# Spreading ScalarE's work over a recurrence, and a sum of powers by another identity

## The reference, cut to what matters

```python
# layer 0, feed-forward: a recurrence over t (3136 steps), all 64 images at once
yt = jax.nn.sigmoid(wx_t + yt @ Vt)
# layer 1, mixer
forget_gate = jax.nn.sigmoid(x_ri @ Wf + bf + 2.0)
input_gate = jax.nn.sigmoid(x_ri @ Wi + bi)
delta = jax.nn.softplus(x_ri @ Wd + bd) * 0.1
scale = 0.95 * jax.nn.sigmoid(mag) / (mag + 1e-08)   # |A| <= 0.95
inp_r = delta[..., :c] * input_gate[..., :c] * Bx_r   # inp_i likewise
def step(h_state, _):                                 # 16 times, h0 = 0
    h_r, h_i = h_state
    Ah_r = Ar * h_r - Ai * h_i
    Ah_i = Ar * h_i + Ai * h_r
    return ((fg_r * Ah_r + inp_r, fg_i * Ah_i + inp_i), None)
```

## Time and profile before

| | |
|---|---|
| time, median of 3 runs (lowest, highest) | 14605.63 us (14566.55, 14616.49) |
| the profiled execution's own time | 14537.58 us |
| its span | 14535.8 us |
| busy: PE, PEld, DVE, ACT, POOL | 79%, 60%, 76%, 68%, 28% |
| granted clock of TensorE, mean | 0.81 |

### The profile page before, as it was taken

How to read it: one execution, slowest core, us unless ns; L and a number is a source line. 1 busy time by engine, 2 the same in 40 slices (tenths; PEclk the granted TensorE clock), 3 DMA queues, 4 the chain that set the end, 5 groups by cost and what they waited for, 6 DMA issues and landing times. The chain is left out here.

```text
span 14535.8 us, 248087 instructions
## 1 busy us (share of the span) xinstructions
PE 11419.5 (79%) x87538; PEld 8744.4 (60%) x87538; DVE 11053.6 (76%) x22880; ACT 9833.3 (68%) x22679; POOL 4012.8 (28%) x3975
## 2 busy tenths in 40 slices
PE   7888888888888867777777777777777547776998
PEld 5666666666666645555555555555555235555888
DVE  6777777777777718999999999999999965554133
ACT  6888888888888846666666666667666567776100
POOL 5444444445444421212111211112121111211000
PEclk9999999999999967777777777777777677777555
DMA  3333333333333321111111111111111133333599
GB/s 69 86 81 82 81 82 87 76 90 73 90 77 86 75 61 41 53 53 53 51 47 52 53 53 53 51 46 53 53 52 40 23 84 94 99 90 89 172 316 309
DMA packets 1967708, 1189.72 MB, mean 82 GB/s; under 512 B 48853, under 2 KB 1900056, under 8 KB 1958436
## 3 DMA queue, kind: packets, MB, share of 16 engines
q1 hardware_dynamic: 1554148, 967.87, 26.3%
q10 hardware_dynamic: 408832, 205.55, 5.0%
q0 software_dynamic: 3648, 2.20, 0.1%
HBM read 708.85 MB, written 466.62 MB: 81 GB/s over the span
## 5 line engine op out<-in xcount | busy, mean ns | idle before, releaser
L1236 PEld LDWEIGHTS s_pW<-s_XU,s_vh 128*128 128x128 f32 x6272 | 1415.7, 261 | 1969.1 <-ACT s_XU L1107 1699.7
L1236 PE MATMUL s_pW<-s_XU,s_vh 128*128 128x64 f32 x6272 | 1493.2, 331 | 1071.4 <-ACT s_XU L1107 1071.4
L1107 ACT ACTIVATE s_XU<-s_pW,s_zb 128x64 f32<-128x64 f32 x3136 | 995.7, 318 | 1788.7 <-PE s_pW L1236 1738.1
L1265 PE MATMUL s_pG<-s_wg,s_XNT 128*128 128x384 f32 (+1 forms) x3200 | 1506.0, 559 | 37.5 <-ACT s_Z L1086 37.5
L832 POOL TENSOR_TENSOR s_rst<-s_var,s_epst 128x16 f32<-128x16 f32 (+1 forms) x100 | 141.7, 1417 | 3906.6 <-DVE s_var L79 3906.6
L408 ACT ACTIVATE KB<-pV,qkb 32x392 f32<-32x392 f32 x2048 | 1190.5, 581 | 25.0 <-PE pV L498 1.1
L248 POOL TENSOR_TENSOR SS<-SS,mx 128x784 f32<-128x784 f32 x512 | 769.5, 1503 | 804.8 <-DVE mx L341 804.6
L1203 PEld LDWEIGHTS s_pY<-s_hident,s_XU 128*128 128x128 f32 (+1 forms) x3200 | 752.2, 305 | 177.7 <-issue 129.6
L1711 PE MATMUL c_pS<-c_OX,c_Wm 64*112 64x128 f32 x3584 | 737.6, 420 | 91.1 <-DVE c_X L1727 76.6
L460 ACT ACTIVATE XH<-XR,nm,rs 112x128 f32<-112x128 f32 x1792 | 733.6, 485 | 92.1 <-POOL nm L267 83.6
L506 PE MATMUL pS<-KB,QT 128*64 128x196 f32 x8192 | 793.7, 336 | 0.0
(11 more groups left out here) (249 smaller groups left out, 31958.3 us busy)
## 6 DMA issues: line engine op xcount, KB each, us to landing
XL<-in_x_dram SPq DMA_DIRECT2D x64, 1568.0 KB, 12.4
XR<-in_x_dram SPq DMA_DIRECT2D x64, 1568.0 KB, 18.0
x_dram<-XR SPq DMA_DIRECT2D x64, 1568.0 KB, 8.1
xh_dram<-XH SPq DMA_DIRECT2D x64, 1568.0 KB, 8.1
r_X<-x_dram SPq DMA_DIRECT2D x64, 1568.0 KB, 14.2
c_X<-x_dram SPq DMA_DIRECT2D x64, 1568.0 KB, 19.4
out_dram<-c_X ACTq DMA_DIRECT2D x64, 1568.0 KB, 13.9
s_XQ<-xh_dram ACTq DMA_DIRECT2D x384, 256.0 KB, 2.8
```

The source lines that it names most:

```text
L1107: act.activation(XU[j % 2][:, t, :], pW[t // R % 2][:, B * (t % R):B * (t % R) + B], ACT.Tanh, bias=zb[:, 0:1], scale=0.5).then_inc(u_sb, 1)
L1236: pe.matmul(pW[t // R % 2][:, B * (t % R):B * (t % R) + B], vh[:], before, start=False, stop=True, skip_group_check=True).then_inc(z_ps, 1)
L1265: pe.matmul(pG[i % 3][0:tc, 0:3 * C], XNT[:, i, 0:tc], wg[:], start=True, stop=True).then_inc(g_ps, 1)
```

## The change

It touches `scan_phase` alone.

1. The table of steps. Normalisation is two images a step over eight steps, from k = 7 (in slot 0 from k = 11). `turn_u` and `residual` of the next group stand at k = 17, 19, 21, 24 and 18, 20, 22, 25; the next chunk's inputs are turned at k = 0, 2, 4, 7 and copied at 1, 3, 5, 8. The copies of the turned normalised rows stand at every second step.
2. The sum of powers: t1 = t^2 - 2d and so on are the traces of M^2, M^4, M^8, M^16; one coefficient comes from their product, the other as a quotient by 1 - t + d. The quotient is Exp(-Ln(2x + 2)) on ACT, at k = 24. DVE has 17 half and 14 full instructions for it in a slot, where it had 12 and 18 (`NV` 25). ACT has 7 squares as before, plus Ln and Exp (`NA` 9), at k = 6, 8, 16, 17, 19, 20, 22 and 24.
3. The inputs of the next chunk are turned into PSUM with images innermost (PE writes at a stride of 4), so that ACT's copy reads in order and writes runs of four.
4. One constant column, and one sign in `par_a`.

```diff
+        TURN_IN = (0, 2, 4, 7)
+        KEEP_IN = (1, 3, 5, 8)
+        TURN_U = (17, 19, 21, 24)
+        KEEP_U = (18, 20, 22, 25)
+        def normal_at(s):
+            return 11 if s == 0 else 7
 (vector)
+                    after(4)
+                    did(dve.tensor_tensor(f0[:, 0], d0, t0, ALU.subtract))
                     dve.wait_ge(sp_d, o * 2 + 2)
...
-                    dve.wait_ge(am, o * NA + 5)
-                    did(dve.scalar_tensor_tensor(t2, d1, 2.0, t2, ALU.mult, ALU.subtract))
...
-                    did(dve.scalar_tensor_tensor(rows(f1), both(t1), 1.0, rows(f1), ALU.add, ALU.mult))
-                    did(dve.tensor_tensor(rows(f1), rows(f1), both(t2), ALU.add))
-                    did(dve.scalar_tensor_tensor(rows(f0), both(f1[:, 0]), 1.0, rows(f0), ALU.add, ALU.mult))
-                    did(dve.tensor_tensor(rows(f0), rows(f0), both(f1[:, 1]), ALU.add))
+                    dve.wait_ge(am, o * NA + 3)
+                    did(dve.scalar_tensor_tensor(t2, d1, -2.0, t2, ALU.mult, ALU.add))
+                    did(dve.tensor_tensor(t1, t0, t1, ALU.mult))
+                    dve.wait_ge(am, o * NA + 5)
+                    did(dve.scalar_tensor_tensor(f1[:, 0], d2, -2.0, f1[:, 0], ALU.mult, ALU.add))
+                    did(dve.tensor_tensor(t2, t2, f1[:, 0], ALU.mult))
+                    did(dve.tensor_tensor(t1, t1, t2, ALU.mult))
+                    dve.wait_ge(am, o * NA + 7)
+                    did(dve.scalar_tensor_tensor(f1[:, 1], d1, -2.0, f1[:, 1], ALU.mult, ALU.add))
...
+                    dve.wait_ge(am, o * NA + 9)
+                    did(dve.scalar_tensor_tensor(f0[:, 0], f1[:, 0], 2.0, f0[:, 0], ALU.add, ALU.mult))
+                    did(dve.scalar_tensor_tensor(t0, t0, -1.0, f0[:, 0], ALU.add, ALU.mult))
+                    did(dve.tensor_tensor(t0, t1, t0, ALU.subtract))
+                    did(dve.tensor_tensor(rows(wv), both(f0[:, 0]), rows(wv), ALU.mult))
+                    did(dve.tensor_tensor(rows(inp), both(t0), rows(inp), ALU.mult))
 (scalar)
-                    if conv and 10 <= k < 10 + NQ:
+                    i = 2 * (k - normal_at(s))
+                    if conv and 0 <= i < OS:
...
+                        if k == 19:
+                            needs(11)
+                            if conv:
+                                act.wait_ge(bx_d, oc + 1)
+                            act.activation(f1[:, 0], t2, ACT.Square).then_inc(am, 1)
...
+                        if k == 24:
+                            act.activation(f0[:, 0], f0[:, 0], ACT.Ln, bias=cols[0:tm, 3:4], scale=2.0).then_inc(am, 1)
+                            act.wait_ge(am, o * NA + 8)
+                            act.activation(f0[:, 0], f0[:, 0], ACT.Exp, scale=-1.0).then_inc(am, 1)
 (tensor)
-                    w = pe.transpose(pX[:, tn * b:tn * b + tn], XQ[i % 2][0:tn, b, :], ident[0:tn, 0:tn])
+                    w = pe.transpose(pX[:, 0:Q * tn].rearrange("c (t b) -> c t b", b=Q)[:, :, b], XQ[i % 2][0:tn, b, :],
+                                     ident[0:tn, 0:tn])
```

More of the change, by code:

```diff
@@ L955, in bounded @@
                 dve.wait_ge(pa_d, b0 + 6)
[L956 removed]
+                dve.scalar_tensor_tensor(pa[:, 4 * HC:5 * HC], s_, 1.0, c_, ALU.mult, ALU.add).then_inc(pa_d, 2)
                 dve.wait_ge(pa_d, b0 + 8)
@@ L1003, in _ @@
                 if o is not None:
-                    after(7)
+                    after(8)
                     turned_by(tm, Wv, inp, a, wp_d, wv_d, o)
-                    dve.wait_ge(am, o * NA + 3)
-                    did(dve.scalar_tensor_tensor(t1, d0, -2.0, t1, ALU.mult, ALU.subtract))
+                    dve.wait_ge(am, o * NA + 1)
+                    did(dve.scalar_tensor_tensor(t1, d0, -2.0, t1, ALU.mult, ALU.add))
                     dve.wait_ge(wv_d, o + 1)
@@ L1022, in _ @@
[L1022 to L1025, removed]
+                    did(dve.scalar_tensor_tensor(f1[:, 0], d2, -2.0, f1[:, 0], ALU.mult, ALU.add))
+                    after(13)
+                    did(dve.tensor_tensor(t2, t2, f1[:, 0], ALU.mult))
@@ L1037, in _ @@
                     after(20)
-                    did(dve.scalar_tensor_tensor(rows(wv), both(f0[:, 0]), 1.0, rows(wv), ALU.add, ALU.mult))
-                    did(dve.scalar_tensor_tensor(rows(inp), both(f0[:, 1]), 1.0, rows(inp), ALU.add, ALU.mult))
-                    after(22)
+                    did(dve.tensor_tensor(t0, t1, t0, ALU.subtract))
+                    did(dve.tensor_tensor(rows(wv), both(f0[:, 0]), rows(wv), ALU.mult))
+                    after(21)
+                    did(dve.tensor_tensor(rows(inp), both(t0), rows(inp), ALU.mult))
@@ L1081, in gate @@
                 if i == 0:
-                    wait(act, dv, (oc - 1) * NV + 9)
+                    wait(act, dv, (oc - 1) * NV + 10)
                 bank = pG[i % 3][0:tc]
@@ L1121, in _ @@
                             wait(act, n_ps, oc * NQ)
-                        for i in range(Q * q, Q * q + Q):
+                        for i in (i, i + 1):
                             w = act.activation(XN[0:tc, i, :], X2[oc % NX][0:tc, i, :], ACT.Identity,
                                                bias=nmr[0:tc, i:i + 1], scale=rst[0:tc, i:i + 1])
-                        w.then_inc(xn_d, 1)
-                    if o is not None and k == 6:
-                        needs(4)
-                        act.activation(t1, t0, ACT.Square).then_inc(am, 1)
-                        act.activation(f0[:, 0], t0, ACT.Square, bias=cols[0:tm, 1:2]).then_inc(am, 1)
-                    if o is not None and k == 8:
-                        act.activation(d1, d0, ACT.Square).then_inc(am, 1)
-                    if o is not None and k == 14:
-                        act.wait_ge(am, o * NA + 3)
-                        act.activation(d2, d1, ACT.Square).then_inc(am, 1)
-                    if scan and s == NO - 2 and k == 25:
-                        act.wait_ge(mag_d, j + 1)
-                        act.activation(sc_[0:size(j)], sa[0:size(j)], ACT.Tanh, scale=0.5).then_inc(th_d, 1)
-                    if conv and 12 <= k < 12 + NQ:
-                        q = k - 12
+                        if i % Q == Q - 1:
+                            w.then_inc(xn_d, 1)
+                    if conv and k - normal_at(s) - 3 in (0, 2, 4, 6):
+                        q = (k - normal_at(s) - 3) // 2
                         act.wait_ge(n_ps, oc * NQ + q + 1)
@@ L1158, in _ @@
+                    if scan and s == NO - 2 and k == 26:
+                        act.wait_ge(mag_d, j + 1)
+                        act.activation(sc_[0:size(j)], sa[0:size(j)], ACT.Tanh, scale=0.5).then_inc(th_d, 1)
                     if conv and k > K - OS:
```

83 lines of the change are left out of this document (45 added, 38 removed).

## The result

| | before | with the change |
|---|---|---|
| time, median of 3 runs (lowest, highest) | 14605.63 us | 15076.17 us (15048.58, 15077.55) |
| the profiled execution's span | 14535.8 us | 15075.9 us |

The account below looks back on a forecast made before the run. DVE's and ACT's lists, almost equally long and touching at a few points, bound the kernel. Ring 347, clock 46 and smaller terms -3 made 390 us on 14,605.6, rounded to 14,990 us; range 14,600 to 15,180.

Parts of the forecast that it names:

- The ring: DVE and ACT waiting on each other through step 19's square and the Exp: 62.5 us, setting the beat; chance 0.64.
- the clock: PE's granted clock falls where PE idles as ACT works, slowing late steps: 2 us a chunk, 46 us in all.
- about 62: ACT's own way round in slot 1, step 19 to step 19, in us.
- the signs named beforehand: Observations to show the forecast right, including DVE waits before L1046 of 4 to 8 us and chunks of 262 to 268.
- Step 24: In the recurrence, two table loads, Ln and Exp on ACT: 4.8 us until the quotient is there.
- rival E: Table switches beside the recurrence cost up to a second load's time: 240 us on top, 15,230 us; chance 0.05.
- From slot 3 to slot 0: Square of step 19 to the next slot's, through slot 3's end and slot 0's normalisation: 72.5 us.
- step 17: In slot 0's normalisation, with `turn_u`, transposes and a gate on PE: about 5 us.
- POOL's result is there by then: In slot 0, normalisation starting at 24.0 us hides ACT's 5.94 us wait for POOL.
- Rival B: PE's clock stays high through most of the slot: 9 us a chunk less, 14,400 us; chance 0.10.
- The 25.5 us for ACT's steps 0 to 16: ACT's early part of slot 1 in its own way round, 26.7 us before.
- The layout: Input copies fall from 1.05 to 0.58 us or stay: 0 in the recurrence, 7 us less at the phase's start.

Follow-up runs that it names:

- e5: The kernel before with the new sum of powers and new layout of turned inputs, keeping the old table of steps: 14879.1 us.
- e6: The kernel before with the new table of steps alone, keeping the old sum of powers and layout: 14865.6 us.
- e1: The changed kernel with squares in place of the Ln and Exp, so their table loads go and the quotient is not computed: 14737.8 us.
- e4: The changed kernel with slot 0's normalisation four images a step at k = 11 to 14: 14986.3 us.
- e12: The changed kernel with the third input turned at k = 5 instead of 4 and copied at 6 instead of 5: 15031.3 us.
- e7: The kernel before with the new layout of the turned inputs alone (PE writes PSUM at a stride of 4): 14574.9 us.

## Why the prediction was right, and where its terms were off

**The ring.** Right in kind, and close in size. From square to square of step 19 (L1166), on ACT's timeline after:

```profile
7018.91 1.06 ACT L1166 ACTIVATE s_f<-s_t 128x1024 f32<-128x1024 f32 x1 [5.63 <-DVE s_t L1030]
...
7096.02 1.06 ACT L1166 ACTIVATE s_f<-s_t 128x1024 f32<-128x1024 f32 x1 [6.80 <-DVE s_t L1030]
...
7159.22 1.05 ACT L1166 ACTIVATE s_f<-s_t 128x1024 f32<-128x1024 f32 x1
...
7223.81 1.06 ACT L1166 ACTIVATE s_f<-s_t 128x1024 f32<-128x1024 f32 x1 [0.93 <-DVE s_t L1030]
...
7288.67 1.06 ACT L1166 ACTIVATE s_f<-s_t 128x1024 f32<-128x1024 f32 x1 [5.68 <-DVE s_t L1030]
```

| from slot to slot | forecast | measured |
|---|---|---|
| 3 to 0 | 72.5 | 77.1 |
| 0 to 1 | 63.1 | 63.2 |
| 1 to 2 | 63.7 | 64.6 |
| 2 to 3 | 65.0 | 64.9 |
| sum | 264.3 (266.3 with the clock) | 269.8 |

In slot 1 that square has no wait: there ACT's own list is as long as the ring, as forecast ("about 62"). The idle time that the ring leaves to DVE fits too. Its waits before L1039 and L1046 are together 24.2 us a chunk (539.8 over 22.3 chunks), where 24.6 were forecast. Of the signs named beforehand, two came otherwise: the wait before L1046 alone is 2.8 us and not 4 to 8 (the rest stands before L1039), and a chunk is 269.4 us and not 262 to 268. The halves (e5, e6) say one thing more, which the prediction did not: each alone makes nearly as long a ring.

**Step 24.** Forecast 4.8 us. ACT in slot 2:

```profile
7233.64 1.28 ACT L1174 ACT_TABLE_LOAD   x1
7234.93 1.15 ACT L1174 ACTIVATE s_f<-s_f,s_cols 128x1024 f32<-128x1024 f32 x1
7236.10 1.28 ACT L1176 ACT_TABLE_LOAD   x1
7237.40 1.06 ACT L1176 ACTIVATE s_f<-s_f 128x1024 f32<-128x1024 f32 x1
```

It is 4.82 from load to the Exp's end (the two functions 0.2 longer together than taken). From t, the start of the square of step 19, to DVE's L1046 it is 15.8 us in slot 1 (forecast 15.1), 14.7 in slot 2 (15.1), 15.5 in slot 0 (15.7) and 11.9 in slot 3 (11.5). e1 confirms the term by removing its loads. The second load starts 0.02 us after the Ln's end, so no drain is paid in the recurrence either. The drain that the Trainium skill (ScalarE: Activation LUTs, What ACT_TABLE_LOAD costs) adds to each switch would, as an estimate, have made this 2.8 us longer; the trace decides against it, and with it rival E fell.

**From slot 3 to slot 0, the terms mis-sized.** 77.1 against 72.5 us. Of the 4.6, 3.3 are slot 3's end: from t to the end of the tanh's load at 7047.24 it is 28.3 us against 25.05. That is the clock, for which I had put 2 us beside the sum. Slot 0 itself makes the other 1.3. These 1.3, the 1.3 by which the clock's 2 us were short and 0.9 us in the other rings make 3.5 us a chunk, 80 of the 86 us by which the forecast was short. In slot 0:

```profile
7045.96 1.28 ACT L1121 ACT_TABLE_LOAD   x1
```

```profile
7062.84 3.19 DVE L924 BATCH_NORM_STATS2 s_st<-s_X 128x6 f32<-128x128 f32 x16 [6.41 <-ACT s_X L1091]
...
7088.03 2.29 DVE L915 TENSOR_TENSOR s_BX<-s_f,s_par_b 128x2048 f32<-128x2048 f32 x1 [10.97 <-ACT s_f L1137]
```

```profile
7074.95 0.88 ACT L1137 ACTIVATE s_f<-s_X,s_nmr,s_rst 128x128 f32<-128x128 f32 x2 [3.93 <-POOL s_nmr L846]
```

From the load's end to `BX` it is 40.8 us, where I had 39.6. Two errors hide in this: the normalisation begins after 27.7 us and not after 24.0, and it lasts 13.1 us and not 15.6, mainly because step 17, taken at about 5 us, took 3.0. That they nearly cancel is luck. The step that failed is "POOL's result is there by then". ACT was ready at 23.8 us, but POOL's result came at 27.7, and ACT's wait stays with 4.1 us a slot 0 (89.1 / 22). The rows of before said as much: there the result came 29.3 us after the load's end, so a start that is later by one step could not hide the wait. It comes 1.6 us earlier now for another reason: DVE reaches its statistics earlier, and they begin 15.6 us after the load's end where it was 17.2. There it waits 6.41 us for the residual's last copy (7062.23), and the statistics and POOL follow it by 12 us. e4, which shortens the normalisation, confirms that slot 0 hangs on it.

**The clock.** 2 us a chunk taken, "none to some four slow steps". Behind step 24 in slot 3 the gates stand up to 1.71 us apart, where a late step takes 0.86:

```profile
7031.21 0.39 ACT L1098 ACTIVATE s_TG<-s_pG 128x256 f32<-128x256 f32 x1
...
7032.32 0.37 ACT L1098 ACTIVATE s_TG<-s_pG 128x256 f32<-128x256 f32 x1
...
7034.03 0.37 ACT L1098 ACTIVATE s_TG<-s_pG 128x256 f32<-128x256 f32 x1
...
7035.74 0.37 ACT L1098 ACTIVATE s_TG<-s_pG 128x256 f32<-128x256 f32 x1
...
7037.44 0.37 ACT L1098 ACTIVATE s_TG<-s_pG 128x256 f32<-128x256 f32 x1
...
7038.79 0.38 ACT L1098 ACTIVATE s_TG<-s_pG 128x256 f32<-128x256 f32 x1
...
7039.66 0.38 ACT L1098 ACTIVATE s_TG<-s_pG 128x256 f32<-128x256 f32 x1
```

These six steps take 8.45 us and not 5.16, so the clock costs 3.3 us behind step 24 in this slot. In the mean of 20 slots 3, e1, where it stays up, gives 2.7 of it back. The windows there show PE busy for 1.08 of 5 us during the loads, then the granted clock (third number from the end) at a mean of 0.57, near 1.2 GHz, and 2.4 again after 7039 us:

```profile
7026.00:7031.00 5.00, 1.08 (x5) 0.46 (x4) 2.18 (x3) 4.96 (x6) 0.00 (x0) 1.00 0.00 0
7031.00:7039.00 8.00, 7.62 (x20) 5.04 (x21) 7.90 (x6) 4.15 (x18) 0.00 (x0) 0.57 0.00 0
7039.00:7044.00 5.00, 5.00 (x23) 3.77 (x22) 4.88 (x3) 4.81 (x10) 0.00 (x0) 1.00 0.00 0
```

Rival B fell with it: the phase's mean stays at 0.76, where it was 0.75.

**DVE.** Forecast 3.06 us less in a slot; it is 2.8 (279.5 over the 100 slots), 11.2 a chunk. The sum took two lengths for a half (1.15 and 1.22). Halves that don't wait for the one before start 1.14 us apart (7044.82 and 7045.96), and those that wait for the one before 1.26 (7020.00, 7021.26, 7022.52), and the new chain has more of these. The saving is worth nothing, because DVE stands idle 41 us a chunk in its place (the four waits of the list, 918.4 us over 22.3 chunks; some 10 before).

**What I had not seen.** With inputs turned at 0, 2 and 4, PE waits for the transfer of the third, 152.1 us in all. e12 got 45 us back by one step. The wait stands in slots 1 to 3. The 25.5 us for ACT's steps 0 to 16 had no room for it; they are 26.3 in slot 1 (7127.31 to 7153.59). How the gain of e12 reaches the rings, where ACT waits for DVE at step 19 anyway, is open. **The layout** behaved as forecast: the copy falls from 1051 to 579 ns and the recurrence gains nothing (e7), since the step was PE's. My reason for a copy that might stay at 1.05 us, "they still write runs of four", misread the kernel before: its copy also read PSUM in order, and it wrote single values 64 values (256 bytes) apart.

```profile
L1083 ACT COPY s_XU<-s_pX 128x512 f32<-128x512 f32 x28 | 16.2, 579 | 0.0
```
